# Attention 2's front in passes: context loaded and transposed first, x in pairs, gates over four batches, scores beside the gate chain

## The chip, the cores and the metric

The kernel runs on one core of a Trainium2 chip. Its engines work side by side and are held together by semaphores alone: PE (TensorE, matmuls and transposes), DVE (VectorE), ACT (ScalarE), POOL (GpSimd) and SP (SyncE, which issues most of the DMAs). The metric is the device time of one execution in microseconds; lower is better.

## The reference

Sixteen batches of 128 tokens, 256 wide, go through four stages, each a residual added to x: attention 1 (cross attention with 16 heads), FFN 1 (fake-quantised), attention 2 (an mLSTM attention with 4 heads, whose keys and values are both the context) and FFN 2 (a mixture of 8 experts). The change concerns attention 2:

```python
# q = layernorm(x); k = v = ctx
gate_in = jnp.concatenate((q, k, v), axis=-1)
ig = gate_in @ igate_kernel + igate_bias        # one value per token and head
fg = gate_in @ fgate_kernel + fgate_bias
def _mlstm_head(q, k, v, ig, fg, eps=1e-06):
    log_f = jax.nn.log_sigmoid(fg)
    cs = concatenate([zeros, cumsum(log_f)])
    log_d = where(tri(s), (cs - cs.T)[1:, 1:] + ig.T, neg)
    m = jnp.max(log_d, axis=-1, keepdims=True)
    d = jnp.exp(log_d - m)
    c = q @ (k.T / sqrt(dh)) * d
    n = maximum(sum(c), exp(-m))
    return c / (n + eps) @ v
```

The scores q k^T of a batch do not depend on the gates. The decay d does, through a cumulative sum and a running maximum along the tokens.

## The kernel before

Everything is written out by hand: each engine has one program, with waits on semaphores placed by hand, so the order of work on an engine is the order of its code, and an engine that waits lets nothing behind the wait go first. x stays in SBUF (x_sb) for the whole kernel. Two large SBUF regions are laid out anew for each stage, so that buffers of different stages share the same place. B is 16 batches, P is 128 tokens, KT is 2 halves of the width, H1 is 4 heads, G is 4 groups of GB = 4 batches.

What lies around the change:

- FFN 1 ends with `down` on PE (L863), DVE scaling its output (L1548), POOL adding it to x (L560, semaphore x2_ready, eight times), DVE taking statistics (L1556, L1561) and POOL taking the root for the norms (L573). POOL then clears q_only and presets v_c (L575, L576).
- The front of attention 2 runs over batches in a two-fold ring. For each batch SP loads its context into ctx_c; DVE normalises x into xn_c (`norm_c`, L1597); PE transposes both halves of x and of the context (`front_c`, L878, L880); ACT copies the result four times (`front_c`, L1178 to L1180): twice into q_only, in which each head has its own rows and zeros elsewhere, once into qT_c, once into ctxT_c; PE forms the gates (`gates_and_scores`, L888, L890: eight rows, 128 tokens) and the scores (L895: four heads times 128), and DVE copies the gates into gates_all (L1602) and the scaled scores into ST (L1604).
- After the last batch comes the gate chain, on (batch, head) rows: SP stores gates_all to DRAM (L422) and loads it back turned into 64 rows (L425); DVE adds the biases (L1629) and readies the soft logarithm (L1631, L1632), ACT takes Exp and Ln (L1193, L1195), DVE goes on with two scans (L1634 to L1641), ACT takes the exponential of the floor (L1198), PE transposes two results (L917, L918), ACT copies them (aT, floorT, L1200, L1201).
- The running maximum, negated, goes to DRAM (L436) and comes back in four DMAs broadcast over all partitions (neg_max, L440). POOL masks it causally, one batch at a time (`causal`, L581), for all 16 batches; only after these come its roots for the loop (`mean_square_root`, L586, L588).
- The loop of attention 2: ACT takes the decays (L1210), DVE multiplies with the scores (L1648), PE multiplies with the values (L928), DVE normalises (L1654 to L1663), POOL takes the root, DVE adds to x (L1668 to L1673), and the router of FFN 2 follows.

## Time and profile before

| | us |
|---|---|
| three runs | 857.07, 858.18, 863.29 |
| median | 858.18 |
| the profiled execution's own time | 865.73 |
| span of its trace | 864.0 |
| granted TensorE clock, mean over the span | 0.879 |
| PE busy | 679.8 (79%) |
| DVE busy | 527.0 (61%) |
| ACT busy | 410.6 (48%) |
| POOL busy | 278.8 (32%) |

Busy time is a sum over the whole kernel, while the change touches one stretch of it, roughly from 270 to 355 us. So the shares tell little here; the rows are read from that stretch: what each engine did at which moment, and what ended each wait. Start times count from the first instruction of the trace.

### The profile page before, as it was taken

Reading aid. Unit: us, or ns where it says so; the run is one execution under the profiler, and the core shown is the slowest. Engines: PE = TensorE matmul, PEld = TensorE weight load, DVE = VectorE, ACT = ScalarE, POOL = GpSimd, SP = SyncE. Lnnn points to the kernel's source line nnn. Section 1 sums busy time; section 2 is a strip of 40 time slices with the busy share of each in tenths; the row PEclk is TensorE's granted clock in tenths of the full one; section 3 lists DMA queues with packets and bytes.
Section 4 is the critical chain, followed back from the end, with each engine's and each line's share of the span. In section 5 each row is a group of like instructions: output and inputs, shape, how many; then the busy total and the mean of one; then the engine's idle time right before and its main releaser. Section 6 shows DMA issues by size and latency. Waiting matters only on the chain.

```text
span 864.0 us, 19336 instructions
## 1 busy us (share of the span) xinstructions
PE 679.8 (79%) x4571; PEld 471.9 (55%) x4615; DVE 527.0 (61%) x1371; ACT 410.6 (48%) x831; POOL 278.8 (32%) x390
## 2 busy tenths in 40 slices
PE   2999999885853991577417989898989998989992
PEld 2788887663322670466404556565656555655661
DVE  5577789985867452788785464646454555464441
ACT  1466655556874463345225444545353545553430
POOL 3111111111436001644302263535354253553421
PEclk9799999986978795555558999999999999999996
DMA  8100000000000114211270514243331525431213
GB/s 260 32 13 12 16 14 13 0 1 1 0 0 12 44 42 159 87 28 27 97 245 19 169 30 132 67 128 73 105 90 31 170 34 165 124 73 24 34 22 110
DMA packets 45844, 58.41 MB, mean 68 GB/s; under 512 B 13497, under 2 KB 39417, under 8 KB 45273
## 3 DMA queue, kind: packets, MB, share of 16 engines
q1 hardware_dynamic: 38328, 47.79, 16.9%
q0 software_dynamic: 7488, 10.31, 7.2%
q8 instruction: 11, 0.18, 0.1%
q14 instruction: 17, 0.13, 0.0%
HBM read 145.90 MB, written 11.80 MB: 183 GB/s over the span
## 4 chain that ended last, share of the span: by engine, by line
PE 48%; DVE 18%; issue 14%; POOL 7%; DMA 3%; ACT 3%; DVEq 2%; POOLq 1%; ACTq 1%; SPq 0%
PE psum L995 16%; PE psum L1017 7%; PE psum L718 3%; PE psum L1008 3%; POOL region L658 3%; PE psum L702 3%; PE psum L725 3%; PE psum L895 2%; PE psum L738 1%; PE psum L757 1%; PE psum L707 1%; PE psum L840 1%; PE psum L888 1%; DVE region L1358 1%; DMA region<-xrow_dram,next_token 1%
## 5 line engine op out<-in xcount | busy, mean ns | idle before, releaser
L995 PE MATMUL psum<-region 128*128 x897 | 209.6, 382 | 19.8 <-POOL pause_p L660 6.2
L995 PEld LDWEIGHTS psum<-region 128*128 128x128 bf16 x936 | 91.6, 98 | 119.1 <-issue 30.4
L1017 PE MATMUL psum<-region 128*128 x936 | 112.5, 278 | 6.2 <-DVE region L1868 3.7
L1017 PEld LDWEIGHTS psum<-region 128*128 128x128 bf16 x936 | 91.3, 100 | 22.3 <-issue 9.2
L1261 ACT ACTIVATE region<-psum 128x512 f32<-128x512 f32 x78 | 46.5, 596 | 115.0 <-PE psum L995 104.2
L1838 DVE TENSOR_TENSOR region<-psum,region 128x512 f32<-128x512 f32 x78 | 53.9, 690 | 72.9 <-ACT region L1261 62.9
L628 POOL TENSOR_TENSOR pause_p<-minus_half 128x1 f32<-128x1 f32 x37 | 7.1, 193 | 191.4 <-DVE next_token L1854 190.6
L640 POOL DMA_INDIRECT sum_dram<-region,tok_idx x39 | 62.0, 1589 | 6.6 <-issue 6.3
L1282 ACT ACTIVATE pause_a<-one_col 128x1 f32<-128x1 f32 x117 | 23.7, 202 | 84.1 <-issue 70.2
L525 POOL TENSOR_TENSOR region<-region,pair_mask 128x256 f32<-128x256 f32 x32 | 18.9, 612 | 137.8 <-ACT region L1062 137.8
L1868 DVE TENSOR_TENSOR region<-psum,region 128x1024 bf16<-128x1024 f32 x39 | 47.6, 1222 | 20.1 <-ACT region L1269 20.1
L629 POOL DMA_INDIRECT region<-xrow_dram,next_token x39 | 41.0, 1051 | 39.6 <-DVE next_token L1833 27.4
L1818 DVE MEMSET pause_d<- 128x1 f32 x80 | 4.7, 59 | 73.5 <-ACT pause_a L1285 40.2
L1269 ACT ACTIVATE region<-psum 128x1024 bf16<-128x1024 f32 x39 | 39.9, 1023 | 16.4 <-PE psum L1008 16.4
L1356 DVE TENSOR_REDUCE region<-psum 128x8 f32<-128x1024 f32 x32 | 39.0, 1218 | 14.1 <-PE psum L718 14.0
L928 PE MATMUL psum<-region 128*128 128x96 f32 x128 | 32.0, 433 | 18.4 <-DVE region L1648 9.2
L1066 ACT ACTIVATE region<-region 128x1024 f32<-128x1024 f32 x32 | 33.8, 1057 | 25.8 <-DVE region L1358 25.8
L1284 ACT ACTIVATE region<-region 128x2048 f32 x24 | 45.8, 1909 | 0.0
L718 PE MATMUL psum<-region 32*128 32x256 f32 x256 | 38.1, 417 | 3.5 <-POOL region L525 3.5
L1820 DVE TENSOR_TENSOR region<-region 128x2048 f32 x17 | 39.0, 2294 | 2.6 <-issue 2.6
L1008 PEld LDWEIGHTS psum<-ident,region 128*128 128x128 f32 x312 | 36.5, 141 | 7.4
L1008 PE MATMUL psum<-ident,region 128*128 128x128 f32 x312 | 40.4, 273 | 0.0
(304 smaller groups left out, 1386.0 us busy)
## 6 DMA issues: line engine op xcount, KB each, us to landing
region<-in_L_ffn_w SPq DMA_DIRECT2D x117, 1024.0 KB
region<-in_ctx SPq DMA_DIRECT2D x48, 128.0 KB, 2.1
region<-neg_max_dram SPq DMA_DIRECT2D x4, 1024.0 KB, 7.6
xrow_dram<-region SPq DMA_DIRECT2D x1, 2080.0 KB, 7.8
x_sb<-in_x SPq DMA_DIRECT2D x4, 512.0 KB, 7.1
sum_dram<-x_sb SPq DMA_DIRECT2D x1, 2048.0 KB, 7.5
region<-in_L_ffn_w_down SPq DMA_DIRECT2D x1, 704.0 KB, 8.1
region<-in_L_ffn_w_gate SPq DMA_DIRECT2D x1, 640.0 KB, 8.6
```

Source lines behind the costliest of these rows:

```text
L629: pool.indirect_dma_start(xg[:, p, :], None, xrow_dram, bass.IndirectOffsetOnAxis(ap=next_token[:, p:p + 1], axis=0)).then_inc(xg_loaded[p ...
L640: pool.indirect_dma_start(sum_dram, bass.IndirectOffsetOnAxis(ap=tok_idx[:, p:p + 1], axis=0), y_d[:, p, :], None, compute_op=ALU.add).the ...
L718: last = mm(S_ps[s][:, 4 * r + 2 * m:4 * r + 2 * m + 2, :], qkT[rows, p, m, :], kbd[rows, p, m, :, :], start=True, stop=True)
L995: last = mm(psum[:, 2 * f + n, :], (xT_lo if xl else xT_hi)[:, p, k, :], weights_at(place, wl, n, k * F1 + f * FH, FH), start=(i == 0), st ...
L1008: last = tr(bank(4, F1 // P, P, count=2)[:, f, :], h_d[:, p, f * P:(f + 1) * P], ident[:])
L1017: last = mm(psum[:, 7, 0:D], (hT_lo if hl else hT_hi)[:, f, :], weights_at(place, wl, 2, f * D, D), start=(i == 0), stop=(i == 3 * (F1 // ...
L1261: act_fn(sil_d[:, f, :], psum[:, 2 * f, :], ACT.Silu).then_inc(sil_d_ready, 1)
L1269: act_fn(hT_hi, bank(4, F1 // P, P, count=2), ACT.Copy).then_inc(hT_high, 1)
L1284: act_fn(expert_w[:, bass.ds(place + n * PART, PART)], stage[:, p, n, :], ACT.Copy)
L1356: nc.vector.tensor_reduce(row_max[:, m, :], S_ps[m][:, :, :], AX.X, ALU.max).then_inc(max_ready, 1)
L1838: tt(h_d[:, p, f * FH:(f + 1) * FH], psum[:, 2 * f + 1, :], sil_d[:, f, :], ALU.mult).then_inc(h_d_ready, 1)
L1868: tt(hT_lo, bank(4, F1 // P, P, count=2), hT_hi, ALU.subtract).then_inc(hT_low, 1)
```

## The change

- SP no longer loads the context batch by batch. Once attention 1 has finished its last product (wo_done), it loads all of it in two DMAs into ctx_all, which lies where attention 1's weights and the later scores (ST) lie. The later half of the batches comes first.
- PE transposes the context in eight pairs of batches (`ctx_transposes`) right after FFN 1's `down`. ACT copies each pair into cT_all, which lies where neg_max lies later. The order of pairs, CTX_PAIRS, is by when FFN 1 leaves each place; the last two pairs (n of 6 and 7) wait for the last residual add.
- x follows in eight pairs (`x_transposes_c`), from a ring of four batches of xn_c, copied into cT_all too. After every second pair PE forms the gates of one group of four batches (`gates`), 512 tokens in one bank. DVE copies them out in four copies (`read_gates`), and SP stores each group as it is ready.
- The scores come last (`scores_c`). ACT fills q_only from cT_all in SBUF (`split_q`), two activations a batch. Their order against the gate chain is set by three numbers: SPLIT_1 = 4 batches before ACT's soft logarithm and DVE's wait for the gates, up to SPLIT_2 = 8 before the exponential of the floor and before DVE's scans, up to SPLIT_PE = 10 before PE's two small transposes, the rest behind them.
- SP issues each of the four neg_max broadcasts only when the scores of its four batches are done, because cT_all lies there. The first values are loaded only when v_c is preset.

PE, from the end of `down` (L863) to the values of attention 2. Before, the first batches; the loop behind repeats them:

```order
L868 COMPARE_AND_BRANCH
L878 MATMUL psum<-ident,region 128x128 x2
L880 MATMUL psum<-ident,region 128x128 x2
L878 MATMUL psum<-ident,region 128x128 x2
L880 MATMUL psum<-ident,region 128x128 x2
L888 MATMUL psum<-region,gk 8x128 x2
L890 MATMUL psum<-region,gk_ctx 8x128 x2
L895 MATMUL psum<-region 128x256 x2
```

Of the change, the same place (L886 is `ctx_transposes`, L895 now `x_transposes_c`, L904 and L906 `gates`, L914 `scores_c`, L929 and L930 the two small transposes):

```order
L886 MATMUL psum<-ident,region 128x128 x32
L895 MATMUL psum<-ident,region 128x128 x12
L904 MATMUL psum<-region,gk 8x512 x2
L906 MATMUL psum<-region,gk_ctx 8x512 x2
L895 MATMUL psum<-ident,region 128x128 x8
...
L895 MATMUL psum<-ident,region 128x128 x4
L904 MATMUL psum<-region,gk 8x512 x2
L906 MATMUL psum<-region,gk_ctx 8x512 x2
L914 MATMUL psum<-region 128x256 x20
L929 MATMUL psum<-ident,region 128x64
L930 MATMUL psum<-ident,region 128x64
L914 MATMUL psum<-region 128x256 x12
```

The context's 32 transposes now stand ahead of everything that needs x, and all 16 batches of scores stand behind the last gates, ten of them ahead of the two small transposes and six behind.

DVE, from the last scores of the front to the floor. Before (L1602 copies gates, L1604 scores; L1629 to L1641 are the gate chain):

```order
L1602 COPY region<-psum 8x128
L1604 TENSOR_SCALAR region<-psum 128x512
L1629 TENSOR_SCALAR region<-region,gbias 64x128 x2
L1631 TENSOR_SCALAR region<-region 64x128
L1632 TENSOR_TENSOR region<-region 64x128
L1634 SCALAR_TENSOR_TENSOR region<-region 64x128
L1636 SCALAR_TENSOR_TENSOR region<-ones_sb,region 64x128
```

Of the change (L1619 `norm_c`, L1624 `read_gates`, L1628 `read_scores`):

```order
L1619 TENSOR_SCALAR region<-x_sb,mv,rstd 128x256 x8
L1624 COPY region<-psum 8x512
L1619 TENSOR_SCALAR region<-x_sb,mv,rstd 128x256 x4
L1624 COPY region<-psum 8x512
L1619 TENSOR_SCALAR region<-x_sb,mv,rstd 128x256 x4
L1624 COPY region<-psum 8x512 x2
L1628 TENSOR_SCALAR region<-psum 128x512 x4
L1652 TENSOR_SCALAR region<-region,gbias 64x128 x2
L1654 TENSOR_SCALAR region<-region 64x128
L1655 TENSOR_TENSOR region<-region 64x128
L1628 TENSOR_SCALAR region<-psum 128x512 x4
L1659 SCALAR_TENSOR_TENSOR region<-region 64x128
```

The copy of a group's gates stands between norms, and four reads of scores stand between the first and the second half of the gate chain; eight more follow the chain.

ACT, behind the evacuations, of the change alone (L1202 is `split_q`, two a batch; L1208 Exp, L1210 Ln, L1215 the floor, L1219 and L1220 the copies of aT and floorT, L1232 the decays). Before, these five stood together and no split stood between them:

```order
L1202 ACTIVATE region<-region 64x2x128 x8
L1208 ACT_TABLE_LOAD
L1208 ACTIVATE region<-region 64x128
L1210 ACT_TABLE_LOAD
L1210 ACTIVATE region<-region,one_col 64x128
L1202 ACTIVATE region<-region 64x2x128 x8
L1215 ACT_TABLE_LOAD
L1215 ACTIVATE region<-region 64x128
L1202 ACTIVATE region<-region 64x2x128 x4
L1219 ACTIVATE region<-psum 128x64
L1220 ACTIVATE region<-psum 128x64
L1202 ACTIVATE region<-region 64x2x128 x12
```

The decays, which open the loop, now stand behind the last twelve of these activations.

The diff, cut to what sets the order of work. On PE, ACT and DVE the removed lines (the old front_c, gates_and_scores and read_gates_and_scores, told above) are left out:

```diff
+    SPLIT_1, SPLIT_2, SPLIT_PE = 4, 8, 10
...
+        (ctx_all,) = lay(region1, (F32, B, D))
+        cT_all = neg_max.rearrange("p (b k) n -> p b k n", k=2 * KT)
+        CTX_PAIRS = (3, 4, 5, 6, 7, 1, 0, 2)
...
+            sp.wait_ge(wo_done, B)
+            ctx_v = ctx_in.rearrange("b p d -> p b d")
             for n in range(2):
-                sp.dma_start(gates_dram[n, :, :, :].rearrange("b h n -> h b n"),
-                             gates_all[n * H1:(n + 1) * H1, :].rearrange("h (b n) -> h b n", n=P)).then_inc(gates_stored, 16)
-            sp.wait_ge(gates_stored, 32)
+                half = slice((1 - n) * B // 2, (2 - n) * B // 2)
+                sp.dma_start(ctx_all[:, half, :], ctx_v[:, half, :]).then_inc(cctx_loaded[n], 16)
+
+            for g in range(G):
+                sp.wait_ge(gates_read, g + 1)
+                for n in range(2):
+                    sp.dma_start(gates_dram[n, g * GB:(g + 1) * GB, :, :].rearrange("b h n -> h b n"),
+                                 gates_all[n * H1:(n + 1) * H1, g * TB:(g + 1) * TB].rearrange("h (b n) -> h b n", n=P)).then_inc(gates_stored, 16)
+            sp.wait_ge(gates_stored, 32 * G)
...
+            sp.wait_ge(q_preset, 2)
...
+                sp.wait_ge(st_done, (g + 1) * GB)
                 sp.dma_start(neg_max[:, rows, :], neg_max_dram[rows, :].unsqueeze(0).to_broadcast([P, GB * H1, P])).then_inc(neg_max_loaded[g], 16)
...
+            def ctx_transposes(n):
+                j = CTX_PAIRS[n]
+                pe.wait_ge(cctx_loaded[0 if j >= B // 4 else 1], 16)
+                if n >= 2:
+                    pe.wait_ge(ct_evac, n - 1)
+                if n == 6:
+                    pe.wait_ge(x2_ready, B // 2)
+                for i in range(2):
+                    for k in range(KT):
+                        last = tr(bank(n % 2, 2, KT, P)[:, i, k, :], ctx_all[:, 2 * j + i, k * P:(k + 1) * P], ident[:])
+                last.then_inc(ct_done, 1)
+
+            def x_transposes_c(j):
+                n = B // 2 + j
+                pe.wait_ge(xn_c_ready, 2 * j + 2)
+                pe.wait_ge(ct_evac, n - 1)
+                for i in range(2):
+                    for k in range(KT):
+                        last = tr(bank(n % 2, 2, KT, P)[:, i, k, :], xn_c[:, (2 * j + i) % 4, k * P:(k + 1) * P], ident[:])
+                last.then_inc(ct_done, 1)
+
+            def gates(g):
+                pe.wait_ge(ct_evac, B // 2 + 2 * g + 2)
+                if g >= 2:
+                    pe.wait_ge(gates_read, g - 1)
+                out_g = psum[0:2 * H1, 2 + g % 2, :]
                 for k in range(KT):
+                    mm(out_g, gk[:, k, :], cT_all[:, g * GB:(g + 1) * GB, k, :], start=(k == 0), stop=False)
                 for k in range(KT):
+                    last = mm(out_g, gk_ctx[:, k, :], cT_all[:, g * GB:(g + 1) * GB, KT + k, :], start=False, stop=(k == KT - 1))
                 last.then_inc(gates_done, 1)
+
+            def scores_c(b, p):
+                pe.wait_ge(ct_evac, B + 2 * b + 2)
+                if b >= 2:
                     pe.wait_ge(st_read, b - 1)
                 for k in range(KT):
+                    last = mm(bank(4 + p, H1, P)[:, 2 * k:2 * k + 2, :], cT_all[:, b, KT + k, :], q_only[:, p, 2 * k:2 * k + 2, :],
                               start=True, stop=True)
                 last.then_inc(st_done, 1)
+            for n in range(B // 2):
+                ctx_transposes(n)
             pe.wait_ge(gk_ready, 1)
+            for j in range(B // 2):
+                x_transposes_c(j)
+                if j >= 2 and j % 2 == 0:
+                    gates(j // 2 - 1)
+            gates(G - 1)
+            for b in range(SPLIT_PE):
+                scores_c(b, b % 2)
             pe.wait_ge(a_ready, 2)
             tr(psum[:, 6, 0:B * H1], gtmp[0:B * H1, 0, :], ident[0:B * H1, 0:B * H1])
             tr(psum[:, 6, B * H1:2 * B * H1], gtmp[0:B * H1, 1, :], ident[0:B * H1, 0:B * H1]).then_inc(aT_done, 1)
+            for b in range(SPLIT_PE, B):
+                scores_c(b, b % 2)
...
+            for n in range(B // 2):
+                j = CTX_PAIRS[n]
+                act.wait_ge(ct_done, n + 1)
+                act_fn(cT_all[:, 2 * j:2 * j + 2, KT:2 * KT, :], bank(n % 2, 2, KT, P), ACT.Copy).then_inc(ct_evac, 1)
+            for j in range(B // 2):
+                n = B // 2 + j
+                act.wait_ge(ct_done, n + 1)
+                act_fn(cT_all[:, 2 * j:2 * j + 2, 0:KT, :], bank(n % 2, 2, KT, P), ACT.Copy).then_inc(ct_evac, 1)
+
+            def split_q(b, p):
+                if b >= 2:
+                    act.wait_ge(st_done, b - 1)
                 for half in range(2):
                     rows = slice(half * HALF, (half + 1) * HALF)
+                    act_fn(q_only[rows, p, half:H1:2, :], cT_all[rows, b, 0:KT, :], ACT.Copy).then_inc(ct_evac, 1)
             act.wait_ge(q_preset, 2)
+            for b in range(SPLIT_1):
+                split_q(b, b % 2)
             act.wait_ge(soft_abs, 1)
             act_fn(lf[0:B * H1, :], lf[0:B * H1, :], ACT.Exp, scale=-1.0).then_inc(soft_log, 1)
             act.wait_ge(soft_log, 1)
             act_fn(lf[0:B * H1, :], lf[0:B * H1, :], ACT.Ln, bias=one_col[0:B * H1, :]).then_inc(soft_log, 1)
+            for b in range(SPLIT_1, SPLIT_2):
+                split_q(b, b % 2)
             act.wait_ge(floor_ready, 1)
             act_fn(gtmp[0:B * H1, 1, :], gsum[0:B * H1, :], ACT.Exp, scale=-1.0).then_inc(a_ready, 1)
+            for b in range(SPLIT_2, SPLIT_PE):
+                split_q(b, b % 2)
             act.wait_ge(aT_done, 1)
             act_fn(aT, psum[:, 6, 0:B * H1], ACT.Copy)
             act_fn(floorT, psum[:, 6, B * H1:2 * B * H1], ACT.Copy, bias=1e-6).then_inc(aT_ready, 1)
+
+            for b in range(SPLIT_PE, B):
+                split_q(b, b % 2)
...
+            def norm_c(b):
+                nc.vector.tensor_scalar(xn_c[:, b % 4, :], x_sb[:, b, :], mv[:, b, 0:1], rstd[:, bass.ds(b, 1)],
                                         ALU.subtract, ALU.mult).then_inc(xn_c_ready, 1)
+            def read_gates(g):
+                dve.wait_ge(gates_done, g + 1)
+                nc.vector.tensor_copy(gates_all[0:2 * H1, g * TB:(g + 1) * TB], psum[0:2 * H1, 2 + g % 2, :]).then_inc(gates_read, 1)
+
+            def read_scores(b, p):
                 dve.wait_ge(st_done, b + 1)
                 nc.vector.tensor_scalar_mul(ST[:, bass.ds(H1 * b, H1), :], bank(4 + p, H1, P), float(DH1) ** -0.5).then_inc(st_read, 1)
+            for b in range(B):
+                if b >= 4 and b % 2 == 0:
+                    dve.wait_ge(ct_done, B // 2 + b // 2 - 1)
+                norm_c(b)
+                if b % GB == 3 and b >= 2 * GB - 1:
+                    read_gates(b // GB - 1)
+            read_gates(G - 1)
+            for b in range(SPLIT_1):
+                read_scores(b, b % 2)
...
             link_c(last)
             link_c(nc.vector.tensor_scalar_mul(lf[0:R, :], gates8[0:R, 1, :], -1.0))
             nc.vector.tensor_tensor(lf[0:R, :], lf[0:R, :], gates8[0:R, 1, :], ALU.max).then_inc(soft_abs, 1)
+            for b in range(SPLIT_1, SPLIT_2):
+                read_scores(b, b % 2)
             dve.wait_ge(soft_log, 2)
             link_c(nc.vector.scalar_tensor_tensor(out=lf[0:R, :], in0=gates8[0:R, 1, :], scalar=0.0, in1=lf[0:R, :],
                                                   op0=ALU.min, op1=ALU.subtract))
...
             link_c(nc.vector.tensor_tensor_scan(gmax[0:R, :], ones_sb[0:R, :], gtmp[0:R, 0, :], NEG, ALU.mult, ALU.max))
             nc.vector.tensor_scalar_mul(ga[0:R, :], gmax[0:R, :], -1.0).then_inc(neg_max_ready, 1)
             nc.vector.tensor_tensor(gsum[0:R, :], gsum[0:R, :], gmax[0:R, :], ALU.add).then_inc(floor_ready, 1)
+            for b in range(SPLIT_2, B):
+                read_scores(b, b % 2)
```

## Rows read from the trace of the kernel before

**Rows 1.** Chain that ended last, 268 to 362 us, shares by line

```profile
by line: PE psum L895 17.9%; PE psum L888 10.1%; issue 9.8%; POOL region L581 8.7%; PE psum L890 7.9%; DMA region<-neg_max_dram 4.8%; PE psum L878 4.2%; PE psum L880 3.9%; DMA gates_dram<-region 3.1%; DMA region<-gates_dram 2.4%; POOL regio
```

**Rows 2.** Chain, same stretch, in order: start us, us, what. Front

```profile
279.97 1.55 DVE region L1597
...
286.34 2.01 PE psum L895 x4
...
296.59 0.22 PE psum L878 x2
...
297.56 0.44 PE psum L890 x4
298.00 1.06 PE psum L895 x4
...
324.74 0.29 DVE region L1602
```

**Rows 3.** Chain, same stretch: gate chain and neg_max

```profile
325.37 2.87 DMA gates_dram<-region
328.26 2.26 DMA region<-gates_dram
...
333.25 0.41 ACT region L1195
333.68 0.29 DVE region L1634
...
335.21 0.23 DVE region L1640
335.46 1.81 DMA neg_max_dram<-region
337.28 4.52 DMA region<-neg_max_dram
...
349.89 2.84 POOL region L581 x4
```

**Rows 4.** Timeline: start, busy us, engine, line, op, xcount, [idle before <-releaser]

```profile
250.42 5.58 PE L863 MATMUL psum<-region 128*128 128x256 bf16 x24 [4.87 <-ACT region L1161]
...
281.76 0.66 PE L878 MATMUL psum<-ident,region 128*128 128x128 f32 x2 [9.29 <-DVE region L1597]
...
336.03 0.37 PE L917 MATMUL psum<-ident,region 64*128 64x64 f32 x1 [10.26 <-ACT region L1198]
...
336.66 0.22 ACT L1201 ACTIVATE region<-psum 128x64 f32<-128x64 f32 x1
...
343.98 0.90 DVE L1648 TENSOR_TENSOR region<-region 128x512 f32<-128x512 f32 x1 [8.35 <-ACT region L1210]
...
354.16 0.43 DVE L1668 TENSOR_TENSOR region<-region 128x256 f32<-128x256 f32 x1 [3.68 <-POOL region L588]
```

**Rows 5.** Windows: length, busy by engine, PEclk third from the end

```profile
255.00:256.00 1.00, 1.00 (x5) 0.40 (x3) 0.00 (x0) 1.00 (x1) 0.88 (x1) 0.55 0.00 0
276.00:277.00 1.00, 0.00 (x0) 0.00 (x0) 0.77 (x5) 0.00 (x0) 1.00 (x2) 0.69 0.00 0
290.00:291.00 1.00, 1.00 (x7) 0.72 (x6) 0.26 (x1) 0.67 (x3) 0.00 (x0) 0.98 0.40 131
362.00:372.00 10.00, 7.69 (x33) 7.03 (x33) 9.30 (x34) 6.00 (x21) 4.64 (x8) 0.50 0.16 37
460.00:461.00 1.00, 1.00 (x5) 0.38 (x4) 0.99 (x1) 0.73 (x3) 0.00 (x0) 0.65 0.00 0
```

**Rows 6.** Chain of the whole span, the start of FFN 2's matmuls

```profile
457.82 3.96 PE psum L995 x11
```

**Rows 7.** Lines by form: busy us, mean ns | idle before; 280 to 326, then ACT's span

```profile
L1604 DVE TENSOR_SCALAR region<-psum 128x512 f32 x14 | 9.7, 691 | 13.0 <-PE psum L895 13.0
...
L1597 DVE TENSOR_SCALAR region<-x_sb,mv,rstd 128x256 f32 x14 | 5.7, 409 | 1.8 <-PE psum L880 1.3
...
L1227 ACT ACTIVATE region<-region 128x256 f32 x10 | 4.1, 406 | 0.0
```

## What the change should do to the time: the prediction

> **What bounds the kernel now.** I read the chain of work that ended last, cut to the stretch from 268 to 362 us, since the change touches only the front of attention 2. The reader is to see which engine carries it: PE's scores (L895), gate products (L888, L890) and transposes (L878, L880) lead the list [rows 1]. In order of time the chain has four parts. First, PE stands idle for 9.29 us after the last matmul of FFN 1, because the first normalised batch is ready only at 281.52 [rows 2, 4]. Second, from 281.76 on PE goes through 16 batches one after the other. Once the clock is at its upper level a batch costs 0.44 (four transposes), 0.44 for each of two pairs of gate products (the row of one pair stands for both) and 1.06 (scores); the last gates are copied out at 325.03 [rows 2]. Third, the gate chain: store 2.87 and load 2.26 through DRAM, the soft logarithm done at 333.66, two scans to 335.44, then 1.81 and 4.52 to store and broadcast neg_max [rows 3]. Fourth, POOL's 16 causal selects end at 352.73, and only behind them stands its root for batch 0, for which DVE has waited 3.68 us, since 350.48 [rows 3, 4]. From there on the loop is untouched. So the gain or loss is the shift of two moments: the end of the last select (352.73), and DVE's readiness (350.48), which comes 6.5 us after its first decay product at 343.98 [rows 4].
>
> **Part 1, context first.** All context is loaded once attention 1 is done, near 190, far ahead. Its 8 pair transposes fall into PE's 9.29 idle: at the low clock four transposes take 4 x 0.22 = 0.88, eight pairs 7.0, and a copy of 512 columns at 0.69 beside each (DVE's row, wider than needed) 5.5. Two pairs wait for the last residual add, but so does the norm at 279.97. Cost nothing; if the cover were gone, at most those two pairs, 1.8 us. It takes two of the four transposes out of each batch, 16 x 0.22 = 3.5 us of PE.
>
> **Part 2, x pairs and gates.** Gate products stream the same columns: 8 x 0.44 = 3.5 us for a group of four batches, so no saving in them. Norms: batch 0 ends at 281.52 as now, the next follow at 0.41 [rows 2, 7]. The second is needed for the first x pair: transposes from 282.1. Pair 2 ends at 285.0 (low clock), where group 0 starts. How long the clock stays low I take from two restarts: PE starts at 250.42 and the mean 0.55 in 255 to 256 puts the rise at 255.9, 5.5 later; it starts at 457.82 and 0.65 in 460 to 461 gives 460.7, 2.9 later [rows 4 to 6]. Where there was a short pause behind the start (281.76, rise at 290.0), 8.2. I take 4.2, between the first two. Low until 286.3: 0.65 of group 0 done, the rest 2.85, end 289.15. Now a wait that the diff adds: DVE's copy of group 0 stands ahead of norms 8 and 9, and x pair 4 ahead of group 1. PE stalls for 0.15 + 0.69 + 2 x 0.41 + 0.2 = 1.86, less what it has to do. Group 1 runs 291.45 to 294.95; the same once more, group 2 ends 300.75; pair 7 and its copy (0.44 + 0.7) stand bare before group 3, which ends at 305.4. Copied out at 306.25, 18.8 earlier than now.
>
> **Part 3, gate chain.** From the last copy to the landed gates now 5.5 us; the last stores are a quarter as large. Between no saving and 1.06 (2.87 becoming the 1.81 of the neg_max store) I take 0.5: 311.25. Then 3.14 as now to the logarithm: 314.4.
>
> **Part 4, the scores beside it.** Scores 0 to 3 follow the gates: 305.4 + 4.24 = 309.65. Splits 4 to 7 stand behind Ln on ACT, two activations of 0.41 each [rows 7]. So score 4 starts at 315.25, after a pause of 5.6. The clock fell 3.9 us after PE's last matmul at 272.47 [rows 4, 5], so it starts low: 4.2 us do half the work, 2.1 of 4.24, the rest 2.14: score 7 ends 321.6. DVE has its reads of scores 4 to 7 ahead of the second half of the gate chain, so that half waits for them: 322.45, against 314.4 for its input. This gives back 8 us of the 18.8. Chain 1.78: 324.2. Exponential 0.59: 324.8. Only then split 8, score 8 from 325.7, after a pause of 4.1, low again: 2 x 2.01 [rows 2], 329.7. Transposes and copies 0.85 [rows 4], split 10 another 0.85: 331.4. Scores 10 to 15 need 6.36 at the high clock. If the short pause lets the low spell go on counting from 325.7, they end at 337.8; if it starts anew, 339.9. I take 338.8.
>
> **Part 5, neg_max.** The store leaves at 324.2; groups 0 and 1 are broadcast at once, but the transposed context lies in neg_max, so group 3 goes only after score 15: 338.85 + 4.52 + 2.84 for the last four selects = 346.2, 6.5 us ahead of 352.73. DVE, free at 338.8 + 0.84, is ready 6.5 later, at 346.15, also no later than POOL. So 6.5 us are gained. The profiled execution took 865.73 around a span of 864.0, 0.9% over the median 858.18; a shift of one stretch carries over whole: 858.2 - 6.5 = **851.7 us**.
>
> The Trainium skill, TensorE: Matmul & The Clock Gate, section on HAM oscillation, says that bursts of matmuls parted by waits each start at half rate again. By that rule both score bursts start low; the trace agrees for the 9.29 us pause. It speaks against leaving PE to wait in the middle of the scores.
>
> **Rivals.** *A, the clock stays high or recovers at once.* For it: the context work keeps PE moving until 280. Against: it fell 3.9 us into a pause. Same sum with no low spell: group 3 ends 303.95, logarithm 312.9, score 7 at 318.0, score 15 at 332.3, last select 339.7: 13.0 earlier, **845.2 us**. Chance 0.20.
>
> *B, the clock stays low through scores 4 to 15.* For it: in 362 to 372 PE is busy 7.69 of 10 us and stays at 0.50 [rows 5], and scores with waits between may look like that. Against: scores 4 to 7 and 10 to 15 run without a gap for 8 us and more. Scores at 2.01: score 7 at 323.3, score 9 at 331.4, score 15 at 345.15, last select 352.55: 0.2 earlier, **858.0 us**. Chance 0.12.
>
> *C, slower: the gates also stay low.* The stalls of 1.86 between groups leave PE about as busy as in that row at 0.50. Each group then takes 7.0; group 3 ends at 320.0, its copy at 320.85, 14.6 later than in my sum, so all of B comes 14.6 later: 14.4 behind now, **872.6 us**. B leaves only 0.2, so any group run low decides for slower, and two and a half of them for more than 1%. Against: the first group and the pairs before it run 7 us unbroken, more than 5.5. Chance 0.05.
>
> *D, POOL's early selects block DVE's reads.* They now run beside the reads of scores 8 to 15. The first norm took 1.55 where later ones took 0.41, beside a POOL memset [rows 2, 7]. If each read of 10 to 15 waited 0.71 for a select, a batch would take 0.69 + 0.71 = 1.4 instead of 1.06: 6 x 0.34 = 2.0 less gain, **853.7 us**. But the read takes its operand from PSUM. Chance 0.03 beside the rest. The Trainium skill, SBUF — State Buffer, on the shared port pair: DVE is locked out only in a two-port mode or with two SBUF inputs. By it the reads are free; no row here shows it.
>
> **Numbers.** Forecast 0.60, A 0.20, B 0.12, C 0.05, D 0.03. With spells of 2.9 and the early end of the scores my own case gives about 849, with spells of 8.2 and the late end 856. The range 845.0 to 858.0 takes in A and B. About 1% (8.6 us, to 849.6) is what a measurement can tell from no change. Faster by more: A and a quarter of the forecast, 0.35. Slower by more: C, 0.05. Within: 0.60.
>
> **What would show it.** In the changed profile: PE transposing from about 272.6; last gate copy near 306; a PE pause of 5 to 6 us behind score 3 and of 4 behind score 7, with the granted clock 0.50 after each; DVE's second half of the gate chain waiting for score 7, not for ACT; the fourth neg_max load issued when score 15 ends; the last select near 346. I am wrong if the clock is 1.00 after those pauses (A), 0.50 through the gates (C), or if the loop behind 352 changes its pace.

## The result, and the profile after

| | before | after |
|---|---|---|
| median of 14 runs each, us | 859.97 | 852.85 |
| lowest to highest, us | 856.38 to 863.29 | 847.97 to 855.71 |
| the profiled execution's own time, us | 865.73 | 855.12 |
| its span, us | 864.0 | 853.4 |
| mean granted TensorE clock in it | 0.879 | 0.888 |

The ratio after to before is 0.9914, with a 95% interval of 0.9896 to 0.9933: 7.1 us by the medians, less than 1%, against a forecast of 6.5 us and 851.7. The two profiled executions differ by 10.6, more than the change is worth; the last section shows where the surplus lies.

Two moments were to move. In the timeline of the changed kernel (start us, busy us, engine, line, operation, tiles, count, idle before and who ended it), POOL's last selects and DVE's first work behind the root, which answer [rows 3] and the last of [rows 4]:

```profile
336.83 3.29 POOL L586 TENSOR_SCALAR_AFFINE_SELECT region<-region 128x512 f32<-128x512 f32 x4 [3.35 <-DMA region<-neg_max_dram]
342.10 2.84 POOL L586 TENSOR_SCALAR_AFFINE_SELECT region<-region 128x512 f32<-128x512 f32 x4 [1.97 <-DMA region<-neg_max_dram]
...
346.36 0.42 DVE L1695 TENSOR_TENSOR region<-region 128x256 f32<-128x256 f32 x1 [3.09 <-POOL region L593]
```

The last select ends at 344.94 where it ended at 352.73, 7.8 earlier, and DVE, ready at 343.27 where it was at 350.48, is 7.2 earlier. The rest of the kernel takes that over nearly whole: the first matmul of FFN 2 (a group of eight, L991 now, L977 before) starts at 438.00 where it started at 445.52, 7.5 earlier. PE's timeline of the changed kernel, from the last context transposes to the last scores, cut to where it waits:

```profile
277.26 1.06 PE L886 MATMUL psum<-ident,region 128*128 128x128 f32 x8 [1.10 <-POOL x_sb L565]
281.69 3.03 PE L895 MATMUL psum<-ident,region 128*128 128x128 f32 x12 [3.36 <-DVE region L1619]
...
290.63 0.66 PE L895 MATMUL psum<-ident,region 128*128 128x128 f32 x4 [0.82 <-DVE region L1619]
...
305.22 4.08 PE L914 MATMUL psum<-region 128*128 128x256 f32 x16
313.96 5.72 PE L914 MATMUL psum<-region 128*128 128x256 f32 x16 [4.66 <-ACT region L1202]
323.42 3.07 PE L914 MATMUL psum<-region 128*128 128x256 f32 x8 [3.73 <-ACT region L1202]
...
328.20 8.85 PE L914 MATMUL psum<-region 128*128 128x256 f32 x24 [1.30 <-ACT region L1202]
```

Four batches of scores take 4.08 at the first burst (305.22) and 5.72 at the second; the last six take 8.85, where the first four's pace would make 6.1. The chain of the same stretch (start, us, what) shows what the second half of the gate chain waits for, and what stands last:

```profile
306.31 1.47 DMA gates_dram<-region
307.80 2.24 DMA region<-gates_dram
...
312.77 0.40 ACT region L1210
...
318.56 1.15 PE psum L914 x4
...
319.73 0.69 DVE region L1628
320.42 0.20 DVE region L1659
...
335.92 1.15 PE psum L914 x4
337.08 4.89 DMA region<-neg_max_dram
```

The soft logarithm is done at 313.17, 20.5 us earlier than the 333.66 of before. DVE's first use of it (L1659) comes at 320.3, because its read of batch 7's scores (L1628) stands ahead of it. The fourth broadcast leaves when score 15 is done. Windows of the clock (length, busy by engine, granted clock third from the end), which answer [rows 5]:

```profile
279.00:280.00 1.00, 0.00 (x0) 0.00 (x0) 0.27 (x1) 0.01 (x1) 1.00 (x2) 0.90 0.00 0
286.00:287.00 1.00, 1.00 (x3) 0.23 (x2) 0.00 (x0) 0.00 (x0) 0.00 (x0) 0.68 0.00 0
314.00:315.00 1.00, 1.00 (x3) 0.82 (x4) 0.00 (x0) 0.77 (x2) 0.00 (x0) 0.50 0.00 0
317.00:318.00 1.00, 1.00 (x5) 0.83 (x5) 0.35 (x1) 0.35 (x1) 0.00 (x0) 0.82 0.00 0
323.00:324.00 1.00, 0.58 (x3) 0.53 (x4) 0.00 (x0) 0.95 (x3) 0.00 (x0) 1.00 0.14 33
324.00:325.00 1.00, 1.00 (x4) 0.77 (x3) 0.18 (x1) 0.24 (x1) 0.00 (x0) 0.59 0.17 66
334.00:335.00 1.00, 1.00 (x5) 0.85 (x4) 0.41 (x1) 0.55 (x2) 0.00 (x0) 0.79 1.10 467
```

A mean of 0.68 between the levels 0.50 and 1.00 puts the rise at 286.64. In the same way the clock fell near 279.8, just before 314.0 and at 324.2, and rose near 286.6, 317.4 and 334.4. So each of the three pauses at 278.3, 309.3 and 319.7 is paid twice in this execution: PE waits, and then runs at 1.2 instead of 2.4 GHz for 5, 3.4 and 10 us.

### The profile page after: what moved, and what is told of

Its sections match the earlier page's. It is cut to its first block, busy times and chain, and to the rows that moved or that the text cites. A ratio compares the mean times of both kernels' runs of the same rounds, so it can differ in the third digit from the quotient of the medians.

```text
span 853.4 us, 18930 instructions
## 1 busy us (share of the span) xinstructions
PE 684.8 (80%) x4518; PEld 465.6 (55%) x4519; DVE 525.0 (62%) x1359; ACT 411.0 (48%) x815; POOL 278.0 (33%) x390
## 4 chain that ended last, share of the span: by engine, by line
PE 49%; DVE 19%; issue 13%; POOL 7%; ACT 3%; DMA 3%; DVEq 2%; POOLq 1%; ACTq 1%; SPq 0%
PE psum L1009 17%; PE psum L1031 7%; PE psum L723 3%; POOL region L663 3%; PE psum L1022 3%; PE psum L707 3%; PE psum L730 3%; PE psum L914 2%; PE psum L743 1%; PE psum L762 1%; PE psum L712 1%; PE psum L845 1%; DMA region<-xrow_dram,next_token 1%; DVE region L1380 1%; PE psum L904 1%
## 5 line engine op out<-in xcount | busy, mean ns | idle before, releaser
L1009 PE MATMUL psum<-region 128*128 x936 | 216.8, 382 | 15.7 <-POOL pause_p L665 6.4
L1031 PE MATMUL psum<-region 128*128 x936 | 112.3, 278 | 6.1 <-DVE region L1895 5.6
L1291 ACT ACTIVATE region<-psum 128x1024 bf16<-128x1024 f32 x39 | 39.9, 1024 | 13.1 <-PE psum L1022 13.1
L1380 DVE TENSOR_TENSOR region<-psum,region 128x1024 f32<-128x1024 f32 x32 | 39.2, 1224 | 1.1
```

Source lines behind the costliest of these rows:

```text
L1009: last = mm(psum[:, 2 * f + n, :], (xT_lo if xl else xT_hi)[:, p, k, :], weights_at(place, wl, n, k * F1 + f * FH, FH), start=(i == 0), st ...
L1031: last = mm(psum[:, 7, 0:D], (hT_lo if hl else hT_hi)[:, f, :], weights_at(place, wl, 2, f * D, D), start=(i == 0), stop=(i == 3 * (F1 // ...
L1291: act_fn(hT_hi, bank(4, F1 // P, P, count=2), ACT.Copy).then_inc(hT_high, 1)
L1380: nc.vector.tensor_tensor(probs[:, m, :, :], S_ps[m][:, :, :], row_max[:, m, :].unsqueeze(2).to_broadcast([P, HT, P]), ALU.subtract).then_ ...
```

## Experiments

The theory to be tested: the gain comes from the gates no longer standing between scores, so that the gate chain starts 19 us earlier, and most of it is given back in three places. (a) The second half of the chain waits for the reads of scores 4 to 7. (b) The score bursts run partly at the low clock, behind pauses. (c) The splits behind ACT's two long activations leave PE waiting. The rival to all of it: what counts is that scores run beside the gate chain, and the series gates, scores, chain would lose the gain.

The first four kernels shared one chip (before: median 859.94, 14 runs), the next four another one (864.91, 17 runs), the last two a third one (860.27, 9 runs). The change's own ratio rests on the runs of the section before (before: 859.97). So they are compared by their ratio to the kernel before. Beside the ratio the table gives the length of the stretch itself in each kernel's profiled execution, from the end of FFN 1's last product on PE to the end of the last select. It leaves out what the stages around it did in that execution.

| kernel | stretch, us | median, us | ratio (95% interval) |
|---|---|---|---|
| before | 80.3 | | 1 |
| the change | 72.7 | 852.85 | 0.9914 (0.9896 to 0.9933) |
| e1_series | 71.4 | 854.45 | 0.9937 (0.9918 to 0.9957) |
| e2_fill | 68.2 | 848.54 | 0.9865 (0.9835 to 0.9896) |
| e3_chain_first | 65.9 | 847.29 | 0.9849 (0.9820 to 0.9878) |
| e4_two_ahead | 64.8 | 847.78 | 0.9867 (0.9840 to 0.9893) |
| e5_ctx_bare | 77.5 | 863.01 | 0.9962 (0.9934 to 0.9991) |
| e6_norms_first | 67.7 | 855.19 | 0.9883 (0.9854 to 0.9913) |
| e7_three | 63.7 | 846.95 | 0.9784 (0.9755 to 0.9812) |
| e8_three_fill | 61.6 | 847.85 | 0.9806 (0.9779 to 0.9834) |
| e9_fill_score | 60.7 | 842.03 | 0.9806 (0.9783 to 0.9830) |
| e10_three_again | 63.4 | 843.62 | 0.9812 (0.9786 to 0.9838) |

**e1_series: scores beside the chain, or in series.**

```diff
-    SPLIT_1, SPLIT_2, SPLIT_PE = 4, 8, 10
+    SPLIT_1, SPLIT_2, SPLIT_PE = 16, 16, 16
```

> All 16 batches of scores stand ahead of the gate chain on ACT, DVE and PE (SPLIT_1 = SPLIT_2 = SPLIT_PE = 16), nothing beside it. My theory: what the changed kernel gains by scores beside the chain it loses by having DVE's second half of the chain wait for score 7 and by two pauses of PE with a low clock behind each. In series the scores run unbroken at the high clock from 305.2 and end at 322.2; then 0.8 for the last read, 1.1 + 2.0 to the logarithm, 1.8 for the scans, 6.4 to the first broadcast neg_max, 10.8 for the selects: 345.1, against 344.9 in the changed kernel. So 853 us, no difference of more than 2 us. Rival, the scores beside the chain are what gains: the 16 us of scores that move ahead of the chain lengthen the path by at least the 11 us between landed gates (310.0) and the soft logarithm's new start less nothing: 860 us or more, no better than the kernel before.

Measured 0.9937, 1.6 us above the change by the medians, with intervals that overlap. PE's scores, DVE's first step of the gate chain and POOL's selects in its timeline:

```profile
300.99 16.52 PE L914 MATMUL psum<-region 128*128 128x256 f32 x64
...
318.17 0.47 DVE L1652 TENSOR_SCALAR region<-region,gbias 64x128 f32<-64x128 f32 x2
...
329.26 10.80 POOL L586 TENSOR_SCALAR_AFFINE_SELECT region<-region 128x512 f32<-128x512 f32 x16 [51.68 <-DMA region<-neg_max_dram]
```

All sixteen scores go in one burst of 16.52 at the high clock. In the change the same work lasts from 305.22 to 337.08, 31.9 us. What the overlap hides, the pauses, the low clock and the late selects cost. So the gain of the change doesn't come from the way in which it lays scores beside the chain; the rival falls.

The first half of the theory falls short too. In e1_series the chain starts only behind all the scores (318.17), and the gain is nearly the same. Its stretch is 8.9 us shorter than before, and the rows say where. PE goes from the end of FFN 1 to its last score in 48.8 us (268.68 to 317.51) where it took 53.3 (272.48 to 325.76), 4.5 less. The chain's first step stands 0.7 behind the last score where it stood 4.8 behind it:

```profile
330.54 0.47 DVE L1629 TENSOR_SCALAR region<-region,gbias 64x128 f32<-64x128 f32 x2 [4.05 <-DMA region<-gates_dram]
```

That line is of the kernel before: DVE waited 4.05 for the trip of the gates through DRAM, which in e1_series goes on beside the scores. These 4.1 and the 4.5 make 8.6 of the 8.9. So what gains there is a shorter front and a hidden trip through DRAM, not an early chain. (Its stretch looks 1.3 us shorter than the change's, but 0.7 of that is a shorter low spell in the front: the first group of gates ended 6.8 us after the first x transposes began, in the change 7.5.)

**e2_fill: the price of the low clock (b).** Matmuls whose result nobody reads keep PE busy in the pauses.

```diff
+            def filler(count):
+                for _ in range(count):
+                    mm(psum[:, 7, 0:P], ident[:], ones_sb[:], start=True, stop=True)
...
                 scores_c(b, b % 2)
+                if b == SPLIT_1 - 1:
+                    filler(16)
+                if b == SPLIT_2 - 1:
+                    filler(12)
...
+            filler(4)
```

> Useless matmuls into an unread PSUM bank fill PE's pauses behind scores 3, 7 and behind the two small transposes (16, 12 and 4 of 0.22 us each), so that the clock has no reason to fall; nothing else is changed. My theory, the low clock of the score bursts costs: score 4 still starts at 313.96, scores 4 to 7 take 4.24 instead of 5.72, the chain follows 1.5 earlier, scores 8 and 9 save another 0.9, scores 10 to 15 save 2.5: score 15 ends about 5.0 earlier, at 332, and the kernel takes 848 us. Rival, the end is set by DMA and selects and PE's clock there costs nothing: 853 us. Second rival, the filler gets in the way of scores that were ready: 855 us.

Measured 0.9865, 848.54 us, 0.5% below the change; the intervals only touch. PE's score bursts now:

```profile
314.32 4.08 PE L918 MATMUL psum<-region 128*128 128x256 f32 x16 [2.44 <-ACT region L1211]
...
322.14 2.01 PE L918 MATMUL psum<-region 128*128 128x256 f32 x8 [1.05 <-ACT region L1211]
...
325.71 6.16 PE L918 MATMUL psum<-region 128*128 128x256 f32 x24 [0.22 <-ACT region L1211]
```

The scores start no sooner than the splits let them; batch 4 even starts 10.1 us behind the start of batch 0 where it was 8.7, because the load of the gates took 3.59 here and 2.24 in the change. But 5.72, 3.07 and 8.85 have become 4.08, 2.01 and 6.16: 5.4 us less PE time, where the medians differ by 4.3. Not all of the 5.4 is the filler's. For the second burst the case is firm: the eight profiles with scores beside the chain and no filler in that pause show 5.48 to 6.65 there, the two with filler 4.08 and 4.05 (this one and e9_fill_score). The other 3.7 us came back without any filler in e6_norms_first below. And five of the change's own 14 runs, 847.97 to 850.62, are about as fast as these six (845.46 to 850.60). So cause (b) is shown as a cost of its own, apart from the waiting, 1.6 us of it by the filler alone; how much of the median it accounts for is not.

**e3_chain_first: the reads ahead of the scans (a).**

```diff
-            for b in range(SPLIT_1, SPLIT_2):
-                read_scores(b, b % 2)
...
-            for b in range(SPLIT_2, B):
+            for b in range(SPLIT_1, B):
                 read_scores(b, b % 2)
```

> DVE's reads of scores 4 to 7 are moved behind the second half of its gate chain; ACT and PE keep their order. My theory, the chain's wait for score 7 gives back 7 us: neg_max is ready at 315.0 instead of 322.1, the second pause of PE (3.7) closes since splits 8 and 9 no longer wait for the floor, score 15 ends at about 330 instead of 337.1, the last select at 337.6: 845.5 us. Rival, the chain is early for nothing because group 3 of neg_max has to wait for score 15 anyway and scores are paced by ACT's splits: score 15 moves by no more than 2, 851 us.

Measured 0.9849, 847.29 us, 0.65% below the change, with intervals apart, and 1.8 us above what I expected. DVE, PE and POOL in its timeline:

```profile
312.22 0.28 DVE L1657 SCALAR_TENSOR_TENSOR region<-region 64x128 f32<-64x128 f32 x1 [2.09 <-ACT region L1210]
...
319.95 2.01 PE L914 MATMUL psum<-region 128*128 128x256 f32 x8 [1.23 <-ACT region L1202]
...
323.54 6.16 PE L914 MATMUL psum<-region 128*128 128x256 f32 x24 [1.30 <-ACT region L1202]
...
334.32 2.84 POOL L586 TENSOR_SCALAR_AFFINE_SELECT region<-region 128x512 f32<-128x512 f32 x4 [0.80 <-DMA region<-neg_max_dram]
```

The second half now follows the logarithm at once, 312.22 instead of 320.33. ACT's exponential of the floor no longer waits, so batch 8's split and scores come earlier; the pause ahead of them shrinks from 3.73 to 1.23, and the clock stays high behind it (2.01 and 6.16). So the reads cost through the wait and, in this execution, through the clock; how much of the second is the edit's is uncertain, since e6_norms_first below kept the clock there too with the full pause of 3.73. Of the 6.8 us by which the stretch is shorter, 3.7 are the two bursts at the high clock, which leaves 3.1 for the wait. Cause (a) is shown; by the medians it is the largest of the three, but its interval overlaps those of e2_fill and e4_two_ahead.

Beside e1_series, on the same chip, this kernel is 7.2 us faster by the medians (847.29 and 854.45, intervals apart). So scores beside the chain are worth much, once nothing stands ahead of the chain's next step on DVE.

**e4_two_ahead: splits further ahead (c).** ACT fills two more batches of q_only ahead of each of its three stops; PE and DVE are unchanged.

```diff
-            for b in range(SPLIT_1):
+            for b in range(SPLIT_1 + 2):
...
-            for b in range(SPLIT_1, SPLIT_2):
+            for b in range(SPLIT_1 + 2, SPLIT_2 + 2):
```

(and the same for the two stretches behind).

> ACT fills q_only two batches further ahead of each step of the gate chain (6 instead of 4 ahead of Exp, 10 instead of 8 ahead of the floor, 12 instead of 10 ahead of the copies); DVE and PE keep their order. My theory: scores 4 and 5 follow score 3 at once, so that PE pauses only about 2.8 behind score 5 for Ln, scores 8 and 9 run beside DVE's scans, and the clock stays high or falls once. Score 15 ends at 327 to 330, last select 335.7 to 338, 844 us (843 to 847). Rival, ACT's longer way to Exp delays the chain by what the scores win: 851 us or more. In both, the chain's wait for score 7 stays.

Measured 0.9867, 847.78 us, 0.5% below the change with intervals just apart, and 3.8 us above what I expected. PE and POOL in its timeline:

```profile
304.29 6.16 PE L914 MATMUL psum<-region 128*128 128x256 f32 x24
313.39 5.48 PE L914 MATMUL psum<-region 128*128 128x256 f32 x16 [2.94 <-ACT region L1202]
...
325.39 10.79 POOL L586 TENSOR_SCALAR_AFFINE_SELECT region<-region 128x512 f32<-128x512 f32 x16 [45.09 <-DMA region<-neg_max_dram]
```

The pause is down to 2.94 us and the clock falls all the same: the burst behind it takes 5.48 instead of 4.08. And with the scores out of the way the selects have become the bound: sixteen in one run of 10.79, which starts only when the first broadcast has landed. Cause (c) is real, but its gain ends at the next bound, the chain that e3_chain_first shortens.

**e5_ctx_bare: what the early context transposes are worth.** PE waits for x before it transposes the context.

```diff
+            pe.wait_ge(gk_ready, 1)
+            pe.wait_ge(xn_c_ready, 2)
             for n in range(B // 2):
                 ctx_transposes(n)
-            pe.wait_ge(gk_ready, 1)
```

> The changed kernel, but PE takes up the context transposes only when the first two batches of x are normalised, so that nothing covers them. My theory, they cost nothing where they stand because PE was idle there: bare, the eight pairs take about 6.5 (five at the low clock, then ACT's pace of 0.7), of which the clock's earlier rise gives back 2.3: the first gate group ends 4.2 later and so does all behind it: 857 us. Rival, the context's place does not matter since PE has slack against DVE's norms or the chain: 853 us. Second rival, what keeps PE moving in the idle time also keeps the clock up, and without it everything is low for longer: 860 us.

Measured 0.9962 where 857 of 860 us, 0.9965, was expected, 0.48% above the change; the intervals (0.9934 and 0.9933 at their near ends) are just apart. PE:

```profile
281.84 6.82 PE L886 MATMUL psum<-ident,region 128*128 128x128 f32 x32 [9.43 <-DVE region L1620]
288.80 1.27 PE L895 MATMUL psum<-ident,region 128*128 128x128 f32 x8
```

The 9.43 us wait of the kernel before is back, and the 6.82 us of context stand bare behind it. The clock rises while they run, at 286.9, so the gates start at the high clock, which pays back part: the first group of gates ends 5.2 later than in the change (294.37 against 289.15, by the start of what follows), not 6.8. So over half of the whole gain, some 4 us with a wide interval, is the context under FFN 1's tail.

**e6_norms_first: the copy of the gates behind the norms.**

```diff
-                if b % GB == 3 and b >= 2 * GB - 1:
-                    read_gates(b // GB - 1)
+                if b in (9, 13, 15):
+                    read_gates((b - 9) // 4 if b < 15 else 2)
```

> The changed kernel, but DVE's copies of gate groups 0 and 1 stand behind the norms of the next two batches (8 and 9, 12 and 13), and that of group 2 behind the last norm, as before. My theory: the two stalls of PE between groups (0.82 each in the profile of the changed kernel) vanish, all behind is 1.6 earlier: 851.2 us. Rival, the stalls are covered by something else that is late (ACT's copies of the x pairs): 853 us.

Measured 0.9883, 0.3% below the change, in the direction expected, but inside the intervals. PE behind the first group of gates:

```profile
288.80 1.10 PE L895 MATMUL psum<-ident,region 128*128 128x128 f32 x8
290.14 1.88 PE L904 MATMUL psum<-region,gk 128*8 128x512 f32 x4 [0.25 <-ACT region L1195]
```

The two x pairs between groups go in one, and the stalls of 0.82 and 0.83 for a norm are gone: group 2 follows group 1 by 4.88 instead of 5.60 us (group 3 follows by 4.87 in both). The trace shows the step; its size in the median isn't resolved. The same profile holds a surprise at the scores, behind the same pause of 3.73 us as in the change:

```profile
321.97 2.01 PE L914 MATMUL psum<-region 128*128 128x256 f32 x8 [3.73 <-ACT region L1202]
...
325.55 6.16 PE L914 MATMUL psum<-region 128*128 128x256 f32 x24 [1.30 <-ACT region L1202]
```

Both bursts ran at a granted clock of 1.00, where the change took 3.07 and 8.85. That alone makes this stretch 3.7 us shorter, of the 5.0 measured.

**e7_three: e3, e4 and e6 together, and e10_three_again.**

> Three reorderings at once: DVE's second half of the gate chain ahead of its reads of scores 4 to 7, ACT's splits two batches further ahead, gate copies behind the next norms. No work is added or taken. My theory: neg_max is ready 8 us earlier than in the changed kernel and score 15 ends 9 to 10 us earlier; the selects, 10.8 for sixteen, start at once and the fourth group waits for score 15 only briefly: last select 9 to 11 earlier, 843 us (841 to 845). Rival, one mechanism stood behind both single reorderings (each gave about 6 us), so that together they give no more than one: 847 us less the 1.6 of the norms, 845.5.

Measured 0.9784 on one chip and 0.9812 on the other, where 843 of 860 us, 0.980, was expected. The rival, one mechanism behind both single gains (845.5 us, 0.983), lies outside the first interval and just inside the second. This is the best version that doesn't rest on filler: about 1.2% below the change, some 2% below the kernel before. PE and POOL in its timeline:

```profile
304.07 6.16 PE L914 MATMUL psum<-region 128*128 128x256 f32 x24
315.11 6.65 PE L914 MATMUL psum<-region 128*128 128x256 f32 x16 [4.88 <-DVE region L1628]
...
333.31 2.84 POOL L586 TENSOR_SCALAR_AFFINE_SELECT region<-region 128x512 f32<-128x512 f32 x4 [1.29 <-DMA region<-neg_max_dram]
```

Batch 6's scores now wait for DVE, whose read of batch 4 stands behind the scans, and again the clock is low for nearly all of the burst behind that pause (6.65). By the ratios the three parts make 0.65, 0.47 and 0.31% alone, 1.4 in sum, and 1.3 and 1.0% together; with intervals of about 0.3 on each side, this neither shows nor excludes that they add up. By the stretch they fall short (6.8, 7.9 and 5.0 us alone, 9.0 together): each single one's profiled execution had escaped the low spell of the last scores (some 6.2 us for the last six in all three, 8.85 in the change), so that its 3.7 us (3.07 + 8.85 against 2.01 + 6.16) stand in each of the three. e6_norms_first escaped it without touching anything there: this spell comes and goes from run to run.

> The kernel of e7_three a second time, on the same chip as e9_fill_score, so that the two are compared side by side and its size rests on two chips. Both theories: 0.978 of the kernel before (0.9755 to 0.9812). If its gain hung on the chip, it would be above 0.983.

**e8_three_fill and e9_fill_score: filler on top.** The kernel of e7_three with 12 filler matmuls behind the context pairs, or with 16 behind the scores of batch 5:

```diff
                 scores_c(b, b % 2)
+                if b == SPLIT_1 + 1:
+                    filler(16)
```

> As the one with three reorderings, with 12 useless matmuls of 0.22 us behind the last context pair, 2.6 of the 3.4 us in which PE waits for the first norms. My theory: the clock does not fall before the gates; 4.9 us of PE's work at the low clock in the changed kernel's profile cost 2.5; in the executions in which the clock stays up anyway nothing is gained. 841.5 us, and a narrower spread of its runs. Rival, the spread comes from FFN 2 and the filler does nothing: 843 us, same spread as the other.

> The three reorderings of e7_three, and 16 filler matmuls (128 x 128, f32, into a bank that nothing reads) behind the scores of batch 5, where PE waited 4.88 us for a read that stands behind the scans. Nothing of the computation is left out. In e7_three the clock fell in that pause and the scores of 6 to 9 took 6.65 us. My theory, that the low clock in the score bursts is a cost of its own: the clock stays 1.00, the four batches take about 4.1, scores 15 ends 2.5 us earlier, and so does the last broadcast; the last select ends near 333.5 of a profile like that one: 2.6 us less than e7_three on the same chip, 0.3%, so a ratio to the kernel before near 0.975. Rival, drawn from e8_three_fill, where a clock kept up at the front showed in the profile and not in the median: another stage gives it back, and the ratio is that of e7_three within 0.1%.

Measured 0.9806 for both, beside 0.9784 (e7_three, same runs as the first) and 0.9812 (e10_three_again, same runs as the second). Score bursts of e9_fill_score, then of e10_three_again:

```profile
309.88 4.05 PE L918 MATMUL psum<-region 128*128 128x256 f32 x16 [1.32 <-DVE region L1634]
```

```profile
314.35 6.53 PE L914 MATMUL psum<-region 128*128 128x256 f32 x16 [4.88 <-DVE region L1628]
```

In the profiles both do what they should: the stretch is 2.1 us shorter than in e7_three and 2.7 shorter than in e10_three_again (2.5 of it in this burst). In the runs the second is 1.6 us faster by the medians, and the first 0.9 slower, its spread (4.1 us) hardly narrower than that of e7_three (4.5). With 5 and 6 runs that spread over 4 to 9 us, 2 us can't be told from nothing: neither the theory (0.3%) nor the rival (given back elsewhere) is refuted. That stays open. The trace gives no sign of a giving back within attention 2: from the last select to the first matmul of FFN 2 it is 93.0 us in both e9_fill_score (328.66 to 421.67) and e10_three_again (335.37 to 428.39), and 93.1 in the change.

## Why the prediction was right, and which terms were off

**The bound and its two moments.** Right. The gain is the shift of the last select (7.8) and of DVE's readiness (7.2; DVE is ready at 343.27, said 346.15, and POOL decides). It is carried over nearly whole: 93.1 us follow before FFN 2 where 92.8 did.

**Part 1, context hidden.** Right. PE transposes from 272.20 to 278.3, beside FFN 1's tail and at the high clock, where the low one was reckoned with, and the first x pair starts at 281.69 (said: 282.1). The value of the cover was put too low in the text: only the last two pairs, 1.8, were named as what is lost without it, while e5_ctx_bare lost some 4 us by moving all eight.

**Part 2, gates.** Right in the sum. The low spell lasted 5 us and not 4.2, group 0 ended at 289.23 (289.15), the stalls were 0.82 where "1.86, less what it has to do" stood, and the last copy ended at 306.0 (306.25).

**Part 3, gate chain.** The store was mis-sized. I took 0.5 off 2.87, from a range that reached to 1.06; it took 1.47, 1.4 off, which is beyond my range: I had let the 1.81 of the neg_max store be the floor, though what is left to store behind the last copy is less than that. The logarithm came 1.2 earlier than said (313.17, 314.4).

**Part 4, the scores beside it.** The order of waits came as said: a pause behind score 3 (4.66, said 5.6), then one behind score 7 (3.73, said 4.1), DVE's second half behind score 7's read. Two sizes were wrong and cancelled in part. A batch of scores at the low clock cost 1.71 in a burst (DVE's reads follow each other at 330.31, 332.01, 333.72) and not the 2.01 of the single row that I took; I had no second row to hold against it, and why that one was longer was not looked into. But the scores from batch 8 on ran at the low clock for 10 us, longer than assumed, and the fall came 0.8 us behind their start; the last ended at 337.08, and the step from 325.7 to 338.8 that I made of 13.1 took 13.7. The gain that this part gives back was put at 8 us, DVE's wait; that wait was 7.2 (313.17 to 320.33). Of it e3_chain_first got back 5.6 by the medians and 6.8 by the stretch, 3.7 of the latter by the clock. And the early chain is not what the gain hangs on: e1_series starts it behind all the scores and gains 5.5 us of its own (859.94 to 854.45).

**Part 5, neg_max.** The fourth broadcast took 4.89 where I carried over 4.52; 344.94 against 346.2.

The terms that came earlier than said (store 1.0, a low score 0.3 each) and those that came later (broadcast 0.4, longer low spells) leave 1.3 us more gain than forecast in the profile, 0.6 by the medians. The order of waits held at every step. That 7.1 comes so near to 6.5 is in part luck: the low spells were 5, 3.4 and 10 us against the one value of 4.2, the low clock cost less per batch than reckoned, and by the bursts of e6_norms_first an execution without the last spell would have shown some 3.7 us more.

**Rivals.** *A, the clock stays high:* refuted for the change, three falls. But the price that it put on the low clock was about right: of its 6.5 us (13.0 against 6.5) 1.5 lie in the front, and the other 5.0 stand beside the 5.4 that the score bursts of e2_fill got back. *B, low through scores 4 to 15:* refuted for this kernel, the clock rose at 317.4 and 334.4. The last burst came near it, low for 6.2 of its 8.85 us. *C, low gates:* refuted, groups 1 to 3 ran at the high clock (3.5 each, as said). *D, selects block the reads:* refuted. The reads L1628 took 0.69 beside the selects from 328 to 337, as everywhere else. The Trainium skill, SBUF — State Buffer, on the shared port pair, has DVE locked out only in a two-port mode or with two SBUF inputs; the trace agrees, and it shows the other side too: the selects took 0.60 on the mean beside these reads (2.40 for four), and 0.82 and 0.71 in the two groups beside some of which DVE's products of two SBUF tiles (L1675) ran (3.29 and 2.84).

**Bursts behind pauses.** In the change, e4_two_ahead and e7_three a pause was followed by a burst at half rate. The Trainium skill, TensorE: Matmul & The Clock Gate, section on HAM oscillation, says that of bursts parted by waits. The traces agree in most places, with two exceptions: the burst at 323.42 in the change began at 1.00 and fell to 0.50 only 0.8 us later, although PE was no longer waiting, and in e6_norms_first the burst behind the same pause of 3.73 us kept 1.00 throughout.

## What to carry to other kernels

When work is laid beside a latency chain, look at what then stands ahead of the chain's own next instruction on each engine: here four reads of an independent product, placed before two scans on DVE, cost nearly all that the overlap was worth (1.6 us over the series with them, 7.2 without), and moving them was a change of three lines. Pauses between matmul bursts should be priced twice, as waiting and as the slower burst that may stand behind them; one long burst in series (16.5 us here) can be nearly as good as an overlap that cuts it into three. And compare a stretch by its own length in the trace beside the median of the whole, since each tells what the other hides.

## What the runs showed of the hardware that was not expected

**The clock fell at no fixed distance from PE's last matmul.** Kernel before, 3.9 us after it [rows 4, 5]; the change, 4.6 in the first pause between scores (309.30 to 313.94) and only 1.5 in the front, behind the last context transposes (278.3 to 279.8); e7_three 4.1; e5_ctx_bare 2.3 (325.55 to 327.82); e4_two_ahead 2.4 (310.45 to 312.88), as the windows of that kernel show:

```profile
312.00:313.00 1.00, 0.00 (x0) 0.00 (x0) 0.00 (x0) 0.96 (x4) 0.00 (x0) 0.94 0.00 0
313.00:314.00 1.00, 0.60 (x2) 0.51 (x3) 0.00 (x0) 0.95 (x3) 0.00 (x0) 0.50 0.00 0
```

The low spells behind it were as uneven: 3.4 us behind the first pause between scores in the change, 10 behind the next, and none behind that pause in e6_norms_first. So my one value of 4.2 for all of them was a poor model: near two of the three spells, far off in the third.

**Runs of one kernel differ by up to 10 us, and the granted clock goes with it.** Of the change's 14 runs the five with a clock of 0.899 or more took 847.97 to 850.62, the nine with 0.894 or less 852.29 to 855.71. In e5_ctx_bare the four runs at 0.897 or more took 856.61 to 857.78, the eight below 861.92 to 866.47. The difference arises also in stages that no edit touches. Ten us of FFN 1, e10_three_again and then e9_fill_score:

```profile
220.00:230.00 10.00, 8.83 (x38) 3.80 (x39) 6.96 (x12) 8.75 (x14) 4.01 (x4) 0.83 0.00 1
```

```profile
220.00:230.00 10.00, 8.85 (x38) 3.22 (x38) 9.13 (x14) 9.06 (x16) 5.29 (x6) 1.00 0.00 1
```

One ran at a mean clock of 0.83 there, the other at 1.00, and the second reached the end of FFN 1 4.0 us sooner (267.97 against 271.95) by the same instructions. Why the same instructions sometimes keep the clock and sometimes lose it was not tried. It is why 2 us could not be settled here. Of the 10.6 us by which the profiled pair differed, 7.5 are the shift of FFN 2's start; the other 3.1 lie behind it, where the two kernels are the same (418.5 us from there to the end before, 415.4 in the change). The mean granted clock there rounds to 0.96 in both, so what made these 3.1 stays open.
